# An attention and MLP kernel: mirrored score blocks turned by VectorE and DMA, and an addition moved to GpSimd

## The chip, the cores and the metric

The kernel runs on one core of a Trainium2 chip. The metric is the device time of one launch in microseconds (us), as the median of several runs. TensorE multiplies, VectorE and ScalarE work on tiles in SBUF (on-chip memory) and PSUM (TensorE's results), GpSimd works on tiles in SBUF, and SyncE issues every DMA of this kernel.

## The reference

The input x has 8 batches of 1024 rows and 256 features. All is float32.

```
h = layernorm(x) * (1 + ca) + sa                 # ca, sa, ga, cb, sb, gb: per batch, from a small matmul
scores = (h * w_lhs) @ (h * w_rhs).T             # 1024 x 1024 per batch
x = x + ga * (softmax(scores, axis=2) @ h)
h = layernorm(x) * (1 + cb) + sb
x = x + gb * (relu(h @ W1 + b1) @ W2 + b2)       # W1: 256 x 1024, W2: 1024 x 256
```

Both factors of the scores are the same rows scaled by feature, so scores[s, t] = scores[t, s]: the score matrix of a batch is symmetric. This is what lets a block be copied from its mirror image.

## The kernel before

The 1024 rows of a batch are 8 tiles of 128, so the scores are 8 by 8 blocks of 128 by 128. In every batch but the first a product is made from split operands: x is cut into a high part (fp32r, names ending in `hi`) and the rest (`lo`), and each product is three matmuls, hi by hi, hi by lo, lo by hi. With two halves of the 256 features a score group is six matmuls. The first batch multiplies float32 operands directly.

Work is named by steps, and each engine runs its own hand-planned list of them, in order: `FIRST_STEPS` (batch 0), `SECOND_STEPS`, `STEPS` (the loop over batches 2 to 6), `LAST_STEPS` and `AFTER_STEPS`. A step with a minus belongs to the batch before, one with a plus to the next. So the MLP of one batch, the attention of the next and the normalisation of a third are interleaved. The steps that matter here:

- `SC.n` (lines 560 to 585, 864): TensorE makes row tile n of the scores in `score[n % 2]` (PSUM); VectorE copies it to `S` and takes the row maxima into `row_max` in the same instruction. Tiles 0 to 3 have all 8 column blocks, tiles 4 to 7 only the 4 right ones. Within the upper left 4 by 4 blocks and within the lower right 4 by 4, the blocks below the diagonal are turned by TensorE (`nc.tensor.transpose`, line 584) from blocks already in `S`, 5 in each; `first_col` makes 11 of 16 be multiplied. With the 16 upper right blocks that is 38 multiplied blocks and 10 turned by TensorE.
- `ST`, `SW`, `SR` and `MX`: the 16 lower left blocks are not made on TensorE. VectorE transposes 32 by 32 pieces of the upper right blocks into `stage` (`ST`, line 896), SyncE stores them to memory (`SW`) and reads them back in turned order into `lower` (`SR`); `MX` (lines 900 and 903) takes their row maxima.
- `MB`: TensorE turns the row maxima into rows in `max_ps`, which is `score[1]` (line 655). `SB.n` (lines 887 to 892): VectorE subtracts the maxima in place in `S`. `EX`: ScalarE's exponential, in place. `SM`: ScalarE writes `Phi` (the high part), VectorE `Plo` (line 911); both are rings of three slots. `AV.n`: TensorE multiplies them with `V`, 24 matmuls; VectorE adds the result to `x_cur` and takes statistics.
- `F.n`, `G.n` (16 each per batch): first and second layer of the MLP. ScalarE makes `hid` and `hid_hi`, and GpSimd `hid_lo` (line 1088), which TensorE needs for the last third of `G.n`. Six matmuls of 512 columns make an `F`, twelve of 256 a `G`.
- `L1`, `L2` (statistics), `N1`, `N2` (normalised rows to `ln_t`), `BH`, `B2`, `TH`, `T2` (turning them by features through VectorE and DMA), `XC` (GpSimd adds the modulation to `x_cur`, line 1139), and `XG` (line 1051): VectorE adds the gated bias `gb_b2` to `x_cur` and writes `x_mlp`.

TensorE's waits that matter: `SC.n` waits until score tile n - 2 is read (`scores_read`), and a turned block until its source is in `S`:

```python
for i in range(left // P, at // P):
    if i == at // P - 1:
        pe.wait_ge(scores_read, T * b + i + 1)
    last = nc.tensor.transpose(score[n % 2][:, i * P:(i + 1) * P], S[:, i, n * P:(n + 1) * P], ident[:])
```

`MB.1` waits for `MX`; `G` waits for `hid_hi` and `hid_lo`; `AV` for `Phi` and `Plo`.

## Time and profile before

| what | value |
|---|---|
| median of 3 runs | 693.37 us (692.94 to 694.24) |
| profiled execution, span from first to last instruction | 691.5 us |
| busy: TensorE, VectorE, ScalarE, GpSimd | 686.1, 558.4, 427.5, 361.7 us |
| TensorE's granted clock, mean | 1.000 (the 2.4 GHz level) |
| DMA | 77.54 MB, 112 GB/s |

The span leaves out what lies before the first and after the last instruction. Busy time of TensorE is from modelled ends of pipelined matmuls, so what a matmul costs is read from the distance between the starts of two, not from its duration.

### The profile page before, as it was taken

Reading aid. Unit: us, or ns where it says so; the run is one execution under the profiler, and the core shown is the slowest. Engines: PE = TensorE matmul, PEld = TensorE weight load, DVE = VectorE, ACT = ScalarE, POOL = GpSimd, SP = SyncE. Lnnn points to the kernel's source line nnn. Section 1 sums busy time; section 2 is a strip of 40 time slices with the busy share of each in tenths; the row PEclk is TensorE's granted clock in tenths of the full one; section 3 lists DMA queues with packets and bytes.
Section 4 is the critical chain, followed back from the end, with each engine's and each line's share of the span. In section 5 each row is a group of like instructions: output and inputs, shape, how many; then the busy total and the mean of one; then the engine's idle time right before and its main releaser. Section 6 shows DMA issues by size and latency. Waiting matters only on the chain.

```text
span 691.5 us, 13488 instructions
## 1 busy us (share of the span) xinstructions
PE 686.1 (99%) x4621; PEld 627.7 (91%) x4621; DVE 558.4 (81%) x1059; ACT 427.5 (62%) x625; POOL 361.7 (52%) x396
## 2 busy tenths in 40 slices
...
GB/s 294 81 49 59 204 193 55 39 107 252 123 100 56 103 232 91 99 61 179 180 67 90 67 226 185 61 38 98 258 121 99 46 91 221 1 1 100 100 31 30
DMA packets 61663, 77.54 MB, mean 112 GB/s; under 512 B 5632, under 2 KB 54336, under 8 KB 61632
## 3 DMA queue, kind: packets, MB, share of 16 engines
...
q14 instruction: 13, 0.11, 0.1%
HBM read 46.15 MB, written 30.97 MB: 112 GB/s over the span
## 4 chain that ended last, share of the span: by engine, by line
PE 94%; DVE 4%; issue 0%; ACT 0%; DMA 0%; DVEq 0%; ACTq 0%; SPq 0%
PE col L595 9%; PE col L594 9%; PE col L593 9%; PE acc L530 8%; PE acc L531 8%; PE acc L536 8%; PE score L694 8%; PE score L690 8%; PE score L691 8%; PE score L578 4%; PE score L579 4%; PE score L580 4%; PE score L576 2%; PE score L584 2%; PE score L499 1%; DVE S L879 1%
## 5 line engine op out<-in xcount | busy, mean ns | idle before, releaser
L1088 POOL TENSOR_TENSOR hid_lo<-hid,hid_hi 128x512 fp32r<-128x512 f32 x127 | 175.4, 1386 | 143.2 <-ACT hid_hi L719 142.8
L715 ACT ACTIVATE hid<-col,b1T 128x512 f32<-128x512 f32 x128 | 87.0, 679 | 140.3 <-PE col L595 126.1
L530 PE MATMUL acc<-W2hi,hid_hi 128*128 128x256 f32 x480 | 119.2, 282 | 0.0
L531 PE MATMUL acc<-W2lo,hid_hi 128*128 128x256 f32 x480 | 116.9, 278 | 0.0
L690 PE MATMUL score<-V,Phi 128*128 128x258 f32 x448 | 108.8, 281 | 0.0
L691 PE MATMUL score<-V,Phi 128*128 128x256 f32 x448 | 108.6, 281 | 0.0
L719 ACT ACTIVATE hid_hi<-hid 128x512 fp32r<-128x512 f32 x128 | 81.0, 633 | 37.6 <-PE acc L536 29.8
L593 PE MATMUL col<-h2hi,W1hi 128*128 128x512 f32 x256 | 102.4, 400 | 0.0
L595 PE MATMUL col<-h2hi,W1lo 128*128 128x512 f32 x256 | 101.0, 395 | 0.0
L594 PE MATMUL col<-h2lo,W1hi 128*128 128x512 f32 x256 | 100.6, 393 | 0.0
L530 PEld LDWEIGHTS acc<-W2hi,hid_hi 128*128 128x128 f32 x480 | 90.4, 188 | 2.1
L531 PEld LDWEIGHTS acc<-W2lo,hid_hi 128*128 128x128 f32 x480 | 90.2, 188 | 1.8
L690 PEld LDWEIGHTS score<-V,Phi 128*128 128x128 f32 x448 | 85.0, 190 | 0.7
L691 PEld LDWEIGHTS score<-V,Phi 128*128 128x128 f32 x448 | 84.0, 188 | 0.6
L1069 POOL TENSOR_SCALAR nm<-mv 128x4 f32<-128x4 f32 x32 | 16.7, 523 | 129.2 <-DVE mv L932 104.2
L911 DVE TENSOR_TENSOR Plo<-S,Phi 128x1024 fp32r<-128x1024 f32 x56 | 70.2, 1269 | 8.1 <-ACT Phi L806 6.4
L536 PE MATMUL acc<-W2hi,hid_lo 128*128 128x256 f32 x480 | 76.6, 276 | 0.0
L864 DVE TENSOR_SCALAR_CACHE_REDUCE S<-score 128x1024 f32<-128x1024 f32 (+1 forms) x64 | 62.7, 980 | 15.2 <-PE score L584 12.9
L793 ACT ACTIVATE S<-S 128x1024 f32<-128x1024 f32 (+1 forms) x64 | 64.4, 1019 | 13.2 <-DVE S L879 7.7
L1139 POOL TENSOR_TENSOR x_cur<-x_cur,attn_mod 128x512 f32<-128x512 f32 x32 | 43.3, 1354 | 40.8 <-DVE ln_v L1038 40.8
L536 PEld LDWEIGHTS acc<-W2hi,hid_lo 128*128 128x128 f32 x480 | 64.6, 188 | 0.0
L694 PE MATMUL score<-V,Plo 128*128 128x258 f32 x448 | 62.8, 282 | 0.0
...
## 6 DMA issues: line engine op xcount, KB each, us to landing
block_rows<-blocks SPq DMA_DIRECT2D x29, 512.0 KB, 2.9
blocks<-block_rows SPq DMA_DIRECT2D x116, 128.0 KB, 3.0
x_cur<-x SPq DMA_DIRECT2D x16, 512.0 KB, 3.9
ln_t<-x SPq DMA_DIRECT2D x14, 512.0 KB, 4.8
score_blocks<-stage SPq DMA_DIRECT2D x14, 512.0 KB, 4.2
lower<-score_blocks SPq DMA_DIRECT2D x56, 128.0 KB, 2.9
out<-x_mlp SPq DMA_DIRECT2D x8, 512.0 KB, 3.0
...
```

The lines of the kernel that those rows point to most:

```text
L530: nc.tensor.matmul(o, hi, W2hi[:, it, :], start=(it == 0 and (apart or t % 2 == 0)), stop=False, skip_group_check=True)
L531: nc.tensor.matmul(o, hi, W2lo[:, it, :], start=False, stop=False, skip_group_check=True)
L536: last = nc.tensor.matmul(o, lo, W2hi[:, it, :], start=False, stop=(it == FT - 1), skip_group_check=True)
L593: nc.tensor.matmul(col[n % 2][:], W1hi[:, kk, tile], h2hi[:, kk, cols], start=(kk == 0), stop=False)
L594: nc.tensor.matmul(col[n % 2][:], W1hi[:, kk, tile], h2lo[:, kk, cols], start=False, stop=False)
L595: last = nc.tensor.matmul(col[n % 2][:], W1lo[:, kk, tile], h2hi[:, kk, cols], start=False, stop=(kk == DK - 1))
L690: nc.tensor.matmul(o, Phi[:, slot, t, :], V[:, t, 0:VW], start=(t == 0), stop=False)
L691: nc.tensor.matmul(o[:, 0:D], Phi[:, slot, t, :], V[:, t, VP:VP + D], start=False, stop=False)
L694: last = nc.tensor.matmul(o, Plo[:, slot, t, :], V[:, t, VP:VP + VW], start=False, stop=(t == T - 1))
L715: nc.scalar.activation(hid[:, n % 2, :], col[n % 2][:], ACT.Relu, bias=b1T[:, n % FT:n % FT + 1]).then_inc(col_read, 1)
L719: nc.scalar.activation(hid_hi[:, n % RING, :], hid[:, n % 2, :], ACT.Copy).then_inc(hid_hi_done, 1)
L1088: G.tensor_tensor(hid_lo[:, n % RING, :], hid[:, n % 2, :], hid_hi[:, n % RING, :].bitcast(F32), ALU.subtract).then_inc(hid_lo_done, 1)
```

## The change

The upper left and lower right 4 by 4 blocks of the scores now have 10 multiplied blocks each, and TensorE turns none (the first batch excepted). The 6 mirrored blocks of each go the way of the lower left ones: `QT` (VectorE, 32 by 32 transposes into `stage_q`), `QW` (store to `quarter_blocks`), `QR` (four reads back). All blocks are packed into `S`; `lower` now lies in `S` too. `SB` no longer works in place: it writes to `soft`, a ring of three slots that lies where `Plo` lies, in three instructions for each row tile. The row maxima are put together from parts (`part_max`), in `MX.0` (upper half, now needed before `MB.0`), `MX.1` (`lower`) and `MX.2` (lower half). `XG` goes from VectorE to GpSimd. All step lists are written anew. The loop's lists, and the first batch's where it matters:

```diff
 FIRST_STEPS
     "pe": """
-        SC.0 MF.2 MF.3 SC.1 MD.0 SC.2 SC.3 SC.4 MB.0 SC.5 SC.6 SC.7 AU.0 AU.1 MB.1 AV.0 AV.1 AV.2 AV.3 AV.4 AV.5
-        AV.6 TP.0 WR.0 AV.7
+        MF.2 SC.0 MF.3 SC.1 MD.0 SC.2 SC.3 SC.4 MB.0 SC.5 SC.6 SC.7 AU.0 MB.1 AU.1 AV.0 AV.1 AV.2 WR.0 AV.3
+        AV.4 AV.5 AV.6 AV.7 TP.0
     "dve": """
-        SC.0 MF.0 L1.0+ SC.1 GA.0 SC.2 BH.0+ SC.3 SC.4 SU.0 SU.1 SC.5 SU.2 SC.6 SC.7 SB.0 SB.1 SU.3 SB.2
+        L1.0+ SC.0 MF.0 BH.0+ GA.0 SC.1 SC.2 SC.3 L1.1+ SC.4 SU.0 SC.5 SC.6 SU.1 SC.7 SU.2 SB.0 SB.1 SB.2 SB.3
 STEPS
     "pe": """
-        SC.0 F.0- SC.1 F.1- F.2- SC.2 SC.3 F.3- SC.4 F.4- MB.0 G.0- SC.5 G.1- SC.6 F.5- SC.7 G.2- F.6- G.3-
-        G.4- F.7- G.5- F.8- F.9- G.6- F.10- MB.1 G.7- AV.0 F.11- AV.1 G.8- F.12- G.9- AV.2 G.10- AV.3 F.13-
-        F.14- AV.4 F.15- G.11- AV.5 G.12- AV.6 G.13- G.14- G.15- AV.7
+        SC.0 SC.1 F.0- F.1- SC.2 SC.3 SC.4 F.2- F.3- SC.5 SC.6 G.0- F.4- SC.7 G.1- F.5- F.6- G.2- G.3- MB.0
+        F.7- G.4- G.5- G.6- G.7- F.8- F.9- F.10- AV.0 G.8- F.11- AV.1 MB.1 G.9- F.12- AV.2 AV.3 AV.4 F.13-
+        G.10- G.11- F.14- AV.5 G.12- F.15- G.13- AV.6 G.14- AV.7 G.15-
     "act": """
+        F.0- VN.0 F.1- T2.1- V.0 F.2- F.3- F.4- VN.1 F.5- V.1 F.6- F.7- EX.0 EX.1 L1.0+ SM.0 F.8- SM.1 F.9-
+        EX.2 F.10- SM.2 EX.3 SM.3 TH.0+ F.11- EX.4 SM.4 EX.5 SM.5 F.12- EX.6 F.13- TH.1+ F.14- EX.7 SM.6 F.15-
+        SM.7 MC.0 T2.0
     "dve": """
-        SC.0 B2.1- ST.0 SC.1 XG.2- ST.1 VL.0 XG.3- SC.2 L1.0+ SC.3 ST.2 ST.3 SC.4 V.0 T2.1- SC.5 SB.0 SB.1
-        SC.6 SC.7 BH.0+ SB.2 VL.1 SM.0 MX.0 SB.3 V.1 L1.1+ SM.1 SB.4 OUT.0- AV.0 BH.1+ SB.5 AV.1 SM.2 SM.3
-        SM.4 TH.0+ SM.5 AV.2 AV.3 SB.6 XG.0 AV.4 B2.0 SB.7 SM.6 TH.1+ AV.5 AV.6 SM.7 T2.0 XG.1 AV.7 OUT.1-
+        B2.1- SC.0 SC.1 ST.0 SC.2 VL.0 SC.3 ST.1 QT.0 ST.2 SC.4 L1.0+ SC.5 SC.6 T2.1- ST.3 SC.7 QT.1 MX.0 V.0
+        VL.1 BH.0+ SB.0 SB.1 MX.1 V.1 SM.0 OUT.0- SM.1 SB.2 L1.1+ MX.2 SB.3 AV.0 SM.2 SM.3 AV.1 BH.1+ SB.4
+        AV.2 SB.5 SM.4 SB.6 AV.3 TH.0+ SB.7 SM.5 B2.0 TH.1+ AV.4 SM.6 AV.5 SM.7 AV.6 AV.7 T2.0 OUT.1-
     "pool": """
-        N2.1- XC.0 F.0- XC.1 F.1- F.2- L1.0+ F.3- N1.0+ F.4- F.5- F.6- XC.2 F.7- F.8- F.9- L1.1+ N1.1+ F.10-
-        F.11- F.12- L2.0 N2.0 XC.3 F.13- F.14- F.15- L2.1
+        N2.1- XG.2- XG.3- F.0- F.1- XC.0 F.2- XC.1 L1.0+ N1.0+ F.3- F.4- F.5- F.6- F.7- F.8- L1.1+ F.9- F.10-
+        N1.1+ F.11- XG.0 L2.0 XG.1 N2.0 XC.2 F.12- F.13- F.14- F.15- XC.3 L2.1
     "sp": """
+        AM.0 S2.1- R2.1- XT.0+ GB.0 X1.0 QW.0 QR.0 SW.0 SW.1 QW.1 SR.0 SR.1 SH.0+ GA.0- RH.0+ XT.1+ QR.1 SH.1+
+        O0.0- RH.1+ S2.0 R2.0 O1.0- X0.0+ O1.1-
 AFTER_STEPS
     "dve": """
-        B2.1- XG.2- XG.3- T2.1- OUT.0- F.15- OT.0-
+        B2.1- T2.1- OUT.0- F.15- OT.0-
     "pool": """
+        N2.1- F.0- F.1- XG.2- XG.3- F.2- F.3- F.4- F.5- F.6- F.7- F.8- F.9- F.10- F.11- F.12- F.13- F.14-
```

The code, cut to its core:

```diff
+    QCOLS = [(0, 1, 2), (1, 2, 3), (2, 3), (0, 3)]
+    UPPER, TURNS = 26, 6
+    PACKED = [0, 3, 6, 8]
+    MAX_ORDER = [3, 0, 1, 2]
...
+                        quarter = QCOLS[n % HT]
+                        for right in range(0 if n < HT else 1, 2):
+                            if right and n == 0:
                                 wait(pe, av_read, T * b)
+                            if not right:
+                                o = score[n % 2][:, 0:HR]
+                            else:
+                                o = score[n % 2][:, HR:HR + len(quarter) * P]
...
-                        for i in range(left // P, at // P):
-                            if i == at // P - 1:
-                                pe.wait_ge(scores_read, T * b + i + 1)
-                            last = nc.tensor.transpose(score[n % 2][:, i * P:(i + 1) * P], S[:, i, n * P:(n + 1) * P], ident[:])
                         last.then_inc(scores_done, 1)
...
                     elif kind == "MB":
-                        pe.wait_ge(scores_read, T * b + HT * (n + 1))
-                        if ph is not PH["first"] and n == 1:
-                            pe.wait_ge(max_ready, b)
+                            pe.wait_ge(max_ready, 2 * b + n - 1)
...
                     elif kind == "SB":
+                        tile, h, t = soft[:, n % RING, :, :], n // HT, n % HT
+                        dve.wait_ge(av_done, T * b + max(n - RING + 1, 0))
...
+                        V_.tensor_tensor(tile[:, h * HT:(h + 1) * HT][:, rows], kept, most.broadcast_to(list(kept.shape)), ALU.subtract)
...
+                        V_.tensor_tensor(by_quarter(out), turned_q[h][:, turns], by_quarter(most.broadcast_to(list(out.shape))), ALU.subtract)
...
+                            V_.tensor_tensor(tile[:, 0:HT], s_upper[:, :, t, :], most.broadcast_to([P, HT, P]), ALU.subtract).then_inc(sub_done, 1)
...
+                    elif kind == "QT":
+                        dve.wait_ge(scores_read, T * b + (n + 1) * HT)
...
+                        V_.transpose(stage_q[n].rearrange("p (u g j r) -> p g j u r", u=Q, g=3, j=2),
+                                     pairs.rearrange("p g j (u r) -> p g j u r", r=QP)).then_inc(quarter_done[n], 1)
+                    elif kind == "MX" and n == 1:
+                        wait_apart(dve, scores_turned[0], 16 * Q * b)
+                        dve.wait_ge(scores_turned[1], 16 * Q * b)
+                        by_row = lower.rearrange("p h u v t r -> p v (h u) (t r)")
+                        V_.tensor_reduce(part_max[:, 1, 3, 0:3], by_row[:, 1:HT], AX.XY, ALU.max)
+                        V_.tensor_reduce(part_max[:, 1, 3, 3:4], by_row[:, 0:1], AX.XY, ALU.max).then_inc(left_done, 1)
                     elif kind == "MX":
+                        h = n // 2
+                        dve.wait_ge(quarter_turned[h], 16 * Q * b)
...
+                        V_.tensor_reduce(places.rearrange("p j g -> p g j"), turned_q[h].rearrange("p (g j) u r -> p g j u r", j=2), AX.XY, ALU.max).then_inc(parts_done, 1)
...
+                        dve.wait_ge(parts_done, 2 * b + h - 1)
+                        V_.tensor_reduce(row_max[:, h * HT:(h + 1) * HT], part_max[:, h].rearrange("p k a -> p a k"), AX.X, ALU.max).then_inc(max_ready, 1)
...
+                    elif kind == "XG":
...
+                        pool.wait_ge(av_read, T * batch + 2 * n + 2)
+                        G.tensor_tensor(x_mlp[:, 2 * n:2 * n + 2, :], x_cur[:, 2 * n:2 * n + 2, :],
+                                        gb_b2[:].unsqueeze(1).broadcast_to([P, 2, D]), ALU.add).then_inc(xg_done, 1)
```

## Rows read from the trace of the kernel before

**Rows 1.** The page: busy time of each engine, and the chain that ended last.

```profile
PE 686.1 (99%) x4621; PEld 627.7 (91%) x4621; DVE 558.4 (81%) x1059; ACT 427.5 (62%) x625; POOL 361.7 (52%) x396
...
PE 94%; DVE 4%; issue 0%; ACT 0%; DMA 0%; DVEq 0%; ACTq 0%; SPq 0%
```

**Rows 2.** One period of the loop: busy us (instructions) by engine, clock, DMA share.

```profile
276.00:358.60 82.60, 82.60 (x576) 76.72 (x575) 71.89 (x133) 54.98 (x81) 45.02 (x49) 1.00 0.38 121
```

**Rows 3.** The timeline of TensorE in batch 4 (from 0): start, duration, line, form.

```profile
319.21 0.34 PE L578 MATMUL score<-Rhi,Lhi 128*128 128x384 f32 x1
...
320.26 0.39 PE L578 MATMUL score<-Rhi,Lhi 128*128 128x512 f32 x1
...
321.64 0.27 PE L584 MATMUL score<-ident,S 128*128 128x128 f32 x1
...
326.61 0.38 PE L584 MATMUL score<-ident,S 128*128 128x128 f32 x2
...
326.95 0.28 PE L579 MATMUL score<-Rlo,Lhi 128*128 128x256 f32 x1
```

**Rows 4.** VectorE's groups by form: busy time, mean ns of one, then idle before.

```profile
L864 DVE TENSOR_SCALAR_CACHE_REDUCE S<-score 128x1024 f32<-128x1024 f32 x36 | 43.7, 1214 | 6.6 <-PE score L584 4.4 <-PE score L576 2.2
L887 DVE TENSOR_TENSOR S<-S,score 128x1024 f32<-128x1024 f32 x28 | 33.3, 1195 | 1.0 <-PE score L655 1.0
...
L1051 DVE TENSOR_TENSOR x_mlp<-x_cur,gb_b 128x512 f32<-128x512 f32 x32 | 24.8, 782 | 3.0 <-DMA out<-x_mlp 3.0
...
L864 DVE TENSOR_SCALAR_CACHE_REDUCE S<-score 128x512 f32<-128x512 f32 x28 | 19.0, 680 | 8.6 <-PE score L584 8.5
L896 DVE STREAM_TRANSPOSE stage<-S 128x512 f32<-128x512 f32 x28 | 19.0, 693 | 0.1
L892 DVE TENSOR_TENSOR S<-lower,score 128x512 f32<-128x512 f32 x28 | 19.0, 677 | 3.9 <-DMA lower<-score_blocks 3.9
...
L900 DVE TENSOR_REDUCE left_max<-lower 128x4 f32<-128x2048 f32 x7 | 15.9, 2272 | 0.0
```

**Rows 5.** GpSimd's groups by form.

```profile
L1088 POOL TENSOR_TENSOR hid_lo<-hid,hid_hi 128x512 fp32r<-128x512 f32 x127 | 175.4, 1386 | 143.2 <-ACT hid_hi L719 142.8
L1139 POOL TENSOR_TENSOR x_cur<-x_cur,attn_mod 128x512 f32<-128x512 f32 x32 | 43.3, 1354 | 40.8 <-DVE ln_v L1038 40.8
L1079 POOL TENSOR_SCALAR ln_t<-x_cur,nm,rs 128x256 f32<-128x256 f32 x64 | 37.8, 606 | 3.4 <-POOL rs L1072 2.3 <-issue 1.0
L1072 POOL TENSOR_TENSOR rs<-var_eps,half_power 128x4 f32<-128x4 f32 x32 | 35.6, 1112 | 2.7
```

**Rows 6.** The timeline of VectorE in batch 4.

```profile
370.58 1.78 DVE L997 SCALAR_TENSOR_TENSOR Llo<-featT,wl,Lhi 128x512 fp32r<-128x512 f32 x1
```

**Rows 7.** The timeline of GpSimd at that time.

```profile
370.09 1.72 POOL L1088 TENSOR_TENSOR hid_lo<-hid,hid_hi 128x512 fp32r<-128x512 f32 x1 [2.78 <-ACT hid_hi L719]
```

**Rows 8.** The page: DMA issues, with KB each and microseconds to landing.

```profile
score_blocks<-stage SPq DMA_DIRECT2D x14, 512.0 KB, 4.2
lower<-score_blocks SPq DMA_DIRECT2D x56, 128.0 KB, 2.9
```

**Rows 9.** The timeline of VectorE in the first batch.

```profile
22.60 1.39 DVE L951 BATCH_NORM_STATS2 stats<-ln_t 128x6 f32<-128x256 f32 x4
...
28.47 0.71 DVE L990 STREAM_TRANSPOSE blocks<-ln_t 128x512 f32<-128x512 f32 x1
```

**Rows 10.** The timeline of TensorE in the first batch.

```profile
24.22 2.75 PE L576 MATMUL score<-R_first,L_first 128*128 128x256 f32 x8
26.81 0.38 PE L584 MATMUL score<-ident,S 128*128 128x128 f32 x2
```

**Rows 11.** Tile ln_t in batch 0: first DMA issue, and times to landing.

```profile
L400 SPq DMA_DIRECT2D ln_t<-x x1: 3960/3960/3960, 6.9 to 6.9; - x1
...
DMA to landing us min/median/max: 4.0/8.3/12.6
```

**Rows 12.** The timeline of TensorE's weight loads at the second batch's start.

```profile
69.38 0.19 PEld L578 LDWEIGHTS score<-Rhi,Lhi 128*128 128x128 f32 x1 [0.55 <-DVE x_cur L926]
```

More of the change, by code:

```diff
@@ L339, in block_kernel @@
         scores_done, scores_read = sem("scores_done"), sem("scores_read")
+        parts_done = sem("parts_done")
         max_done, left_done, max_ready = sem("max_done"), sem("left_done"), sem("max_ready")
-        stage_done, stage_stored, scores_turned = sem("stage_done"), sem("stage_stored"), sem("scores_turned")
+        stage_done, stage_stored, scores_turned = sem("stage_done"), [sem("stage_stored0"), sem("stage_stored1")], [sem("scores_turned0"), sem("scores_turned1")]
+        quarter_done, quarter_stored, quarter_turned = [[sem(f"quarter_{what}{h}") for h in range(2)] for what in ("done", "stored", "turned")]
         sub_done, exp_done, phi_done, plo_done = sem("sub_done"), sem("exp_done"), sem("phi_done"), sem("plo_done")
@@ L559, in part @@
                             pe.wait_ge(scores_read, T * b + n - 1)
[L560 to L570 removed]
+                        tile = slice(n * P, (n + 1) * P)
@@ new lines, in part @@
+                        if ph is PH["first"]:
+                            at = first_col[n]
+                            for lo_col in range(0, ROWS, HR):
+                                start_col = max(at, lo_col)
+                                width = lo_col + HR - start_col
+                                if width <= 0 or n == 0 and lo_col == 0:
+                                    continue
+                                o, cols = score[n % 2][:, start_col:lo_col + HR], slice(start_col, lo_col + HR)
+                                for kk in range(DK):
+                                    last = nc.tensor.matmul(o, L_first[:, kk, tile], R_first[:, kk, cols], start=(kk == 0), stop=(kk == DK - 1))
+                            for i in range(at // P):
+                                if i == at // P - 1:
+                                    pe.wait_ge(scores_read, T * b + i + 1)
+                                last = nc.tensor.transpose(score[n % 2][:, i * P:(i + 1) * P], S[:, i, n * P:(n + 1) * P], ident[:])
+                            last.then_inc(scores_done, 1)
+                            continue
```

233 lines of the change are left out of this document (133 added, 100 removed).

## The prediction

> **What bounds the kernel now.** I read the page first, for who is busy and what the last chain is made of: TensorE is busy 99% of the span and makes 94% of the chain [rows 1]. Both could hide short waits, because ends of matmuls are modelled, so the second view is a window of about one loop period: TensorE 82.60 of 82.60 us at clock 1.00, VectorE 71.9, GpSimd 45.0 [rows 2]. The third is the timeline inside a batch, where starts follow each other in fixed steps with no wait between them [rows 3]. So in the loop the time is TensorE's instruction list, and each nanosecond taken from that list is won, as long as what feeds TensorE stays ahead of it. VectorE has some 10.7 us of idle time in a period to do so, GpSimd 37.6.
>
> **TensorE's list.** Six matmuls of 384 columns run from 319.21 to 320.26, 0.175 us each, and six of 512 from 320.26 to 321.64, 0.230 each [rows 3]; by that line one of 256 takes 0.12. The change narrows the right group of `SC.0` and the only group of `SC.4` from four blocks to three: 12 matmuls by 0.055 = 0.66 us per batch. The other tiles keep their widths (3 and 4, 2 and 4, 2 and 4, 3, 2, 2 blocks); that the two blocks of `SC.3` and `SC.7` now lie apart I cost at nothing, since the columns stream at the same count, and at up to 12 matmuls by 0.06 = 0.7 if the gap costs half. The ten transposes go: two and the 256-column matmul behind them take 326.61 to 326.95, 0.34 less 0.12, so 0.11 each [rows 3], 1.10 us per batch. Together 1.76, in seven batches 12.3 us. Both parts lie on TensorE's own list, so nothing has to be found that they uncover. If the transposes were hidden in some pipeline, only 4.6 would be left; the starts say that they aren't.
>
> **VectorE's load.** Lengths by the rows of 512 and 1024 elements, which give about 0.16 us plus 1.03 ns per element [rows 4]. `SC`: four of 1.214 and four of 0.680, 7.58, become 896, 896, 768, 512 and 256, 384, 384, 256, 256 elements: 6.1, so -1.5. `QT`: two transposes of 768, by the row of 693 ns for 512 0.95 each, +1.9 (its four-step pattern could make it 1.8 each, +3.6). `MX`: 2.27 and a small one become 768 twice, 1536, 512 and two small ones, +2.3. `SB`: 4 x 1.35 + 4 x 1.195 = 10.2 become eight of three pieces (0.84 for the two short ones, 0.68), 12.2, +2.0. `XG`: 4 x 0.78 leave, -3.1. Net +1.6 us: 73.5 busy in a period of 80.8. It fits, with 7 us left where 10.7 were.
>
> **GpSimd's load.** Four `XG` at the 1.354 of its other addition of the same shape [rows 5] are +5.4: 50.4 of 80.8. None of it is on TensorE's path by itself; what is queued behind each is. `XG.2` and `XG.3` stand ahead of the first `F`, and TensorE wants that hid_lo only in `G.0`, after seven score tiles and four `F`. `XG.1` is different, see below.
>
> A GpSimd instruction can also hold VectorE up. One `Llo` of 512 columns with two SBUF inputs took 1.78 us [rows 6] while GpSimd worked from 370.09 to 371.81 [rows 7]; the `XG` on VectorE, of the same size with two such inputs, takes 0.78 [rows 4]. So a moved `XG` may give VectorE up to 1.0 us of delay each, 4.0 per period at worst, 0 at best. I take 1 to 2 us per period, inside the 7 left. The Trainium skill has this as a rule (SBUF — State Buffer, section "SBUF: two separate sides"): GpSimd and a VectorE instruction with two SBUF inputs lock one port pair and the loser waits for the whole of the other; the 1.78 agrees with it. By that rule moving additions between the two engines wins VectorE less than its 3.1 us, which speaks against this part of the change.
>
> **The waits that the change adds.** Times from the start of `SC.0`: `F` is six 512-column matmuls, 1.38; `G` twelve of 256, 1.4; `AV` 24 of 256, 2.9.
> - `MB.0` now waits for turned blocks. TensorE reaches it after 12.6 us of scores, seven `F` and four `G`: 27.9. `QT.0` stands behind the read of `SC.3`, done at about 15; the store lands 4.2 later and the reads, 2.9 to land [rows 8] with some 1.5 for issuing four, at 23.6; `MX.0` ends at 24.8. Slack 3. Behind `MX.0` on VectorE stand `V.0`, `VL.1`, `BH.0` and `SB.0`; a late landing would push them all.
> - SyncE gets two stores and eight reads more per batch, placed ahead of `SH.0+`, `RH.0+`; the only one in a hurry is `QR.0`, above. DMA is at a share of 0.38 [rows 2] and gets 1.5 MB more per batch on about 10. I cost it at nothing.
> - `MB.1` comes at 48.1. From `MB.0` on VectorE has about 17 us of listed work up to `MX.2`, and waits for ScalarE's `SM.1` in it: 45. Slack 3.
> - `G.12` is the tightest. GpSimd's list there is `L2.0 XG.1 N2.0 XC.2 F.12-`, and `L2.0` waits for the statistics of `AV.3`. From the end of `AV.3` VectorE has `SM.4`, `SB.6` and its own step, about 4 us; then GpSimd needs at least 1.1, 1.35, four of 0.61, 1.35 and 1.39 [rows 5], 7.6. TensorE wants hid_lo two thirds into `G.12`: `AV.4`, four steps, `AV.5` and 0.9, 12.3 us after `AV.3`. 11.6 against 12.3: slack 0.7. `XG.1` alone is 1.35 of this. ScalarE's `F.14` waits for the same hid_lo, and behind it `EX.7` and `SM.6` for `AV.6`.
> - The ring `soft`: `SB.n` waits for `AV.n-3`, as `Phi` and `Plo` did; at least two `AV` and two `F` or `G` lie between, 8 us, for a chain of 1.5 + 1.0 + 1.0 + 1.2. It costs nothing.
>
> **First and last batch.** In the first, `L1.0+` and `BH.0+` are moved ahead of the reads of `SC.0` and `SC.1`. The first `ln_t` load is issued at 6.85, and with the longest landing of 12.6 [rows 11] is there at 19.5. From its statistics to the transpose of `BH` took 28.47 - 22.60 = 5.9 us [rows 9], so `BH.0` can start at 25.4, ends at 26.7, `GA.0` follows, and `SC.1` is read by 28.2. TensorE wants that for the transposes of `SC.2`, which ran at 26.81 behind eight matmuls from 24.22 [rows 10]. So 1.4 us are lost; up to 3 if `L1.1+`, moved ahead of the read of `SC.4`, is late too; 0 if the load lands in the shortest 4.0. Given back at its end: 0.55 us in which TensorE waited for the read of `AV.7` [rows 12] are filled by `TP.0`, now behind it. Net +0.9 (-0.6 to +2.5). In the last part `G.0` waits for `XG.3`, now behind `N2.1`, two `F` and `XG.2` on GpSimd, 8 us against six `F`, 8.3: nothing, at worst 1.
>
> **Sum.** -12.3 + 0.9 = -11.4. The profiled span is 691.5, so 680.1; the median of the runs lies 1.9 above the span, and so 682.0 is the forecast.
>
> **Rivals.**
> - A, the list shrinks and TensorE stays fed: 682.0, own range 680.3 to 684. Chance 0.62.
> - B, one place per period slips, `G.12` most likely, because `XG.1` or VectorE blocked behind GpSimd eats its slack of 0.7. For it: the 1.78 [rows 6]. Against it: one slip moves TensorE, and all that waits on it gains the same slack, so a period loses once. Six or seven periods by 0.4 to 1.3 us: 684.5 to 690.5. Chance 0.25. This is what the Trainium skill's rule above would make of it.
> - C, slower: VectorE becomes the bound between `QT.1` and `SB.4`. Its 7 us left must be used up and 1.76 more: this takes `QT` at 1.8 each (+1.7), the reduces at twice their 2.3 (+2.3), the short pieces of `SB` at twice their length (+4), and blocking over 1 us. All of it with 3 us of blocking is +11.0, a period of 84.5 us, 1.9 more than the 82.6 of before, seven times: 693.4 + 13.3, about 707. It decides from +9.1 (7.3 left and 1.76). Against it: all rows of these forms lie on one line per element [rows 4]. Chance 0.07.
> - D, only the narrower matmuls count: the transposes' 7.7 stay as some other wait, 689.7. Chance 0.04.
> - E, more than the sum: under 680.3, where the first batch loses nothing and its end wins. Chance 0.02.
>
> **How the numbers follow.** A change of 0.2%, 1.4 us, is about what a measurement of this kernel can tell from none. Faster takes A, B, D, E and little of C: 0.92; same 0.03; slower 0.05. The range leaves out C, E and the top of B: 680.3 to 688.
>
> **What the profile would show.** Right: no transposes on TensorE between the scores after the first batch; 168 score matmuls of 384 columns where 84 were; starts in the same steps of 0.23, 0.175, 0.12; the period shorter by 1.7 to 1.8 us; `XG` on GpSimd at about 1.35 and VectorE at 73 to 76 per period. Wrong: steps between TensorE's starts of over 0.4 us, in `G.12` (waiting for hid_lo), at `MB.0` or `MB.1` (for `MX`), or in `AV` (for `Plo`); in the first batch a pause before the transposes of `SC.2` shows that term. What would upset the forecast most is GpSimd late by over a microsecond in every batch, or `QT` and `MX` far above their lines.

## The result and the profile after

The change makes the kernel slower: 760.6 us median of four runs (759.3 to 761.5), against 693.3 of the kernel before on the same chip (692.9 to 694.2). The ratio is 1.096 [1.0945, 1.0979], 67 us more where 11 less were forecast. The profiled execution has a span of 757.5 us and a mean granted clock of 0.982.

The page of the changed kernel, busy time by engine and what the last chain is made of, answers to [rows 1]:

```profile
PE 699.6 (92%) x4551; PEld 633.7 (84%) x4551; DVE 615.7 (81%) x1168; ACT 429.8 (57%) x625; POOL 422.5 (56%) x428
...
PE 8%; POOL 1%; DVE 0%; issue 0%
```

The chain that was TensorE to 94% breaks off after 9% of the span. TensorE's share of busy time is 92%, with fewer instructions, and the engine now has pauses. VectorE's load rose by 57.3 us, 8.2 a batch. One period, from 250 us, and then three slices of 5 us in it (columns as in [rows 2]):

```profile
250.00:340.70 90.70, 83.39 (x564) 75.99 (x563) 81.47 (x149) 55.20 (x81) 53.37 (x53) 1.00 0.41 127
330.00:335.00 5.00, 3.33 (x28) 3.14 (x28) 3.03 (x4) 1.67 (x3) 5.00 (x7) 1.00 0.18 72
335.00:340.00 5.00, 3.11 (x21) 2.67 (x21) 4.84 (x6) 4.86 (x8) 3.76 (x3) 1.00 0.41 138
340.00:345.00 5.00, 5.00 (x31) 5.00 (x31) 4.63 (x8) 2.78 (x4) 1.47 (x2) 0.66 0.00 0
```

TensorE's list was 82.60 of 82.60 busy; now a period takes about 91 us. TensorE's timeline over that window, the rows that carry a wait (in brackets the idle time before, and its releaser):

```profile
252.20 1.22 PE L746 MATMUL score<-V,Plo 128*128 128x258 f32 x8 [0.73 <-DVE Plo L1015]
...
277.21 0.38 PE L629 MATMUL score<-Rhi,Lhi 128*128 128x256 f32 x1 [1.19 <-DVE S L931]
...
288.50 0.74 PE L569 MATMUL acc<-W2hi,hid_lo 128*128 128x256 f32 x4 [0.43 <-POOL hid_lo L1183]
294.38 0.38 PE L563 MATMUL acc<-W2hi,hid_hi 128*128 128x256 f32 x1 [0.57 <-ACT hid_hi L771]
...
320.27 0.39 PE L742 MATMUL score<-V,Phi 128*128 128x258 f32 x1 [0.57 <-ACT Phi L864]
334.36 0.73 PE L569 MATMUL acc<-W2hi,hid_lo 128*128 128x256 f32 x4 [1.67 <-POOL hid_lo L1183]
339.74 0.38 PE L742 MATMUL score<-V,Phi 128*128 128x258 f32 x1 [1.89 <-DVE x_cur L1032]
```

With one of 0.18 at 295.76, eight waits make 7.2 us. Six kinds of feeder are late in one period: `Plo`, the read of a score tile, `hid_lo`, `hid_hi`, `Phi` and `x_cur`. Two in a row, in `G.12` and at `AV.6`, leave TensorE idle for 3.6 us of ten; from 340 to 345 the granted clock is 0.66, so part of that slice ran at 1.2 GHz and not at 2.4 (the starts of `AV.6`'s matmuls are 0.12 us apart up to 340.4 and 0.21 behind it). Over the whole kernel TensorE's waits after 60 us sum to 48 us, where the kernel before shows none. The mean clock of 0.982 stands for at most 14 us more (757.5 x 0.018); before it was 1.000. What was late there is seen on GpSimd and VectorE:

```profile
324.75 0.52 POOL L1164 TENSOR_SCALAR nm<-mv 128x4 f32<-128x4 f32 x1 [1.70 <-DVE mv L1036]
325.34 0.60 POOL L1165 TENSOR_SCALAR var_eps<-mv 128x4 f32<-128x4 f32 x1
326.02 1.40 POOL L1167 TENSOR_TENSOR rs<-var_eps,half_power 128x4 f32<-128x4 f32 x1
327.40 1.30 POOL L1244 TENSOR_TENSOR x_mlp<-x_cur,gb_b 128x512 f32<-128x512 f32 x1
328.70 3.14 POOL L1174 TENSOR_SCALAR ln_t<-x_cur,nm,rs 128x256 f32<-128x256 f32 x4
331.80 1.28 POOL L1234 TENSOR_TENSOR x_cur<-x_cur,attn_mod 128x512 f32<-128x512 f32 x1
333.04 4.68 POOL L1183 TENSOR_TENSOR hid_lo<-hid,hid_hi 128x512 fp32r<-128x512 f32 x3
```

```profile
331.97 0.71 DVE L1094 STREAM_TRANSPOSE blocks<-ln_t 128x512 f32<-128x512 f32 x1 [2.18 <-POOL ln_t L1174]
332.61 0.67 DVE L1095 STREAM_TRANSPOSE blocks<-ln_t 128x512 f32<-128x512 f32 x1
333.20 1.65 DVE L1101 SCALAR_TENSOR_TENSOR Llo<-featT,wl,Lhi 128x512 fp32r<-128x512 f32 x1
334.77 1.78 DVE L1103 SCALAR_TENSOR_TENSOR Rlo<-featT,wr,Rhi 128x512 fp32r<-128x512 f32 x1
336.48 1.78 DVE L1101 SCALAR_TENSOR_TENSOR Llo<-featT,wl,Lhi 128x512 fp32r<-128x512 f32 x1
338.19 0.74 DVE L1103 SCALAR_TENSOR_TENSOR Rlo<-featT,wr,Rhi 128x512 fp32r<-128x512 f32 x1
```

The reader is to see one chain run back and forth. `L2.0` waits for VectorE's statistics, `XG.1` and a slow `N2.0` follow it, VectorE stands 2.18 us at `B2.0` for that `ln_t`, GpSimd's overdue `hid_lo` burst then runs beside VectorE's `TH.1` and three of its four operations take 1.65 to 1.78 us where the last, beside an idle GpSimd, takes 0.74; the read of `AV.4` behind them is late, and `AV.6` waits for its bank. VectorE's groups by form, for [rows 4], and GpSimd's, for [rows 5]:

```profile
L1015 DVE TENSOR_TENSOR Plo<-soft,Phi 128x1024 fp32r<-128x1024 f32 x56 | 86.1, 1546 | 3.0 <-ACT Phi L864 2.9
L1142 DVE SCALAR_TENSOR_TENSOR ln_v<-ln_v,rs,attn_mod 128x256 f32<-128x256 f32 x56 | 52.9, 1003 | 6.6 <-ACT ln_v L835 5.5 <-DMA attn_mod<-mod_rows 1.1
...
L1006 DVE TENSOR_REDUCE part_max<-S 128x6 f32<-128x768 f32 x14 | 12.9, 925 | 0.0
L999 DVE TENSOR_REDUCE part_max<-S 128x3 f32<-128x1536 f32 x7 | 12.2, 1736 | 0.0
...
L992 DVE STREAM_TRANSPOSE stage_lr<-S 128x768 f32<-128x768 f32 x7 | 6.8, 975 | 0.2
```

```profile
L1174 POOL TENSOR_SCALAR ln_t<-ln_t,nm,rs 128x256 f32<-128x256 f32 x56 | 47.2, 854 | 1.3 <-POOL rs L1167 1.3
...
L1244 POOL TENSOR_TENSOR x_mlp<-x_cur,gb_b 128x512 f32<-128x512 f32 x32 | 44.2, 1390 | 37.2 <-DMA out<-x_mlp 37.2
```

The new operations have the lengths that were forecast (925, 1736, 975 ns; `XG` 1390). The old ones grew. In the same view of the kernel before `Plo` has a mean of 1269 ns and `ln_v` of 498:

```profile
L911 DVE TENSOR_TENSOR Plo<-S,Phi 128x1024 fp32r<-128x1024 f32 x56 | 70.2, 1269 | 8.1 <-ACT Phi L806 6.4 <-issue 0.8
...
L1038 DVE SCALAR_TENSOR_TENSOR ln_v<-ln_v,rs,attn_mod 128x256 f32<-128x256 f32 x56 | 24.5, 498 | 0.5 <-ACT ln_v L783 0.4
```

These two alone are 44.3 us more, at the same count and shape.

In the first batch the forecast term is there. TensorE waits before the second transpose of `SC.2`, for the read of `SC.1`, where none was [rows 10]:

```profile
28.39 0.33 PE L607 MATMUL score<-ident,S 128*128 128x128 f32 x1 [1.07 <-DVE S L924]
...
54.12 12.19 PE L735 MATMUL score<-V_unsplit,S 128*128 128x258 f32 x48 [3.43 <-POOL W2lo L1211]
...
73.90 0.48 PE L629 MATMUL score<-Rhi,Lhi 128*128 128x512 f32 x1
```

The last row is the first score matmul of batch 1. It came at 67.64 before, so the first batch lost 6.3 us, and the wait at `SC.2` is the smaller part of it; the larger is 3.43 us for `W2lo`, in the row between, and behind it the granted clock is 0.66 from 53 to 58 us, some 1.7 us more. From there to the first score matmul of batch 7 the kernel takes 549.0 us for 495.6, 8.9 a period, and from that to its end 134.6 for 128.3. Together 66.0 us, the whole difference of the spans.

### The profile page after: what moved, and what is told of

Same layout as the page of the kernel before. It is cut to its first block and busy times, and to the rows that moved or that the text cites. A ratio compares the mean times of both kernels' runs of the same rounds, so it can differ in the third digit from the quotient of the medians.

```text
span 757.5 us, 13573 instructions
## 1 busy us (share of the span) xinstructions
PE 699.6 (92%) x4551; PEld 633.7 (84%) x4551; DVE 615.7 (81%) x1168; ACT 429.8 (57%) x625; POOL 422.5 (56%) x428
## 5 line engine op out<-in xcount | busy, mean ns | idle before, releaser
L742 PE MATMUL score<-V,Phi 128*128 128x258 f32 x448 | 112.7, 288 | 11.7 <-DVE x_cur L1032 9.4
L743 PE MATMUL score<-V,Phi 128*128 128x256 f32 x448 | 111.8, 286 | 0.0
L742 PEld LDWEIGHTS score<-V,Phi 128*128 128x128 f32 x448 | 87.2, 195 | 14.9 <-issue 10.6
L569 PE MATMUL acc<-W2hi,hid_lo 128*128 128x256 f32 x480 | 79.9, 284 | 13.9 <-POOL hid_lo L1183 13.7
L1015 DVE TENSOR_TENSOR Plo<-soft,Phi 128x1024 fp32r<-128x1024 f32 x56 | 86.1, 1546 | 3.0 <-ACT Phi L864 2.9
L743 PEld LDWEIGHTS score<-V,Phi 128*128 128x128 f32 x448 | 86.5, 193 | 1.1
L1164 POOL TENSOR_SCALAR nm<-mv 128x4 f32<-128x4 f32 x32 | 12.8, 399 | 129.8 <-DVE mv L1036 76.6
L848 ACT ACTIVATE soft<-soft 128x1024 f32<-128x1024 f32 x56 | 58.5, 1053 | 44.1 <-DVE soft L978 24.2
L746 PE MATMUL score<-V,Plo 128*128 128x258 f32 x448 | 65.2, 289 | 5.8 <-DVE Plo L1015 5.8
L629 PE MATMUL score<-Rhi,Lhi 128*128 128x512 f32 (+2 forms) x168 | 58.3, 347 | 8.5 <-DVE S L931 5.0
L1244 POOL TENSOR_TENSOR x_mlp<-x_cur,gb_b 128x512 f32<-128x512 f32 x32 | 44.2, 1390 | 37.2 <-DMA out<-x_mlp 37.2
```

Of the source, the lines that this page charges most:

```text
L569: last = nc.tensor.matmul(o, lo, W2hi[:, it, :], start=False, stop=(it == FT - 1), skip_group_check=True)
L742: nc.tensor.matmul(o, Phi[:, slot, t, :], V[:, t, 0:VW], start=(t == 0), stop=False)
L743: nc.tensor.matmul(o[:, 0:D], Phi[:, slot, t, :], V[:, t, VP:VP + D], start=False, stop=False)
L1015: V_.tensor_tensor(Plo[:, n % RING, :, :], soft[:, n % RING, :, :], Phi[:, n % RING, :, :].bitcast(F32), ALU.subtract).then_inc(plo_done, 1)
```

## The experiments

Three theories were put to the chip: the additions on GpSimd hold the others up (1); the new scheme for the scores does, with its turned quarters and VectorE's added load (2); the new order of the steps does, on all five queues (3). The diff rewrites the order lists together with the scheme, so they had to be taken apart. All runs were timed beside the kernel before, which lay between 693.6 and 694.1 each time.

**The additions.** First the changed kernel with `XG` back on VectorE, and the kernel before with `XG` on GpSimd:

```diff
-"dve":  ... SC.1 ST.0 SC.2 VL.0 ...
-"pool": N2.1- XG.2- XG.3- F.0- ... F.11- XG.0 L2.0 XG.1 N2.0
+"dve":  ... SC.1 XG.2- ST.0 SC.2 VL.0 XG.3- ... SM.5 XG.0 ... SM.7 XG.1
+"pool": N2.1- F.0- ... F.11- L2.0 N2.0
```

> The changed kernel, with the gated bias added on VectorE again (at the places that correspond to the old ones) and everything else as changed. Theory 1: moving the addition to GpSimd is what makes it slow, because it stands in GpSimd's queue waiting for a store, and the work behind it then comes in bursts that hold up VectorE's instructions with two SBUF inputs. Then most of the 67 us come back: 685 to 710 us, and the mean of the ln_v instruction falls from 1003 ns towards 500. Theory 2: the turned blocks and the subtraction out of place cost it, through VectorE and the DMA. Then it stays at 745 or above. Theory 3: the new order of steps on all engines costs it, whoever adds the bias. Then it stays above 735 as well, with the same places of waiting.

Measured: 751.4 us (749.3 to 757.8), 9.2 less than the changed kernel; ratio to before 1.085 [1.080, 1.091]. Its trace has one wait that the changed kernel has at 1.80 us only: `F.0-` in batch 2's list waits 9.19 us for `h2lo`. TensorE's, VectorE's and SyncE's rows:

```profile
174.12 0.79 PE L640 MATMUL col<-h2hi,W1hi 128*128 128x512 f32 x1 [9.19 <-DVE h2lo L1106]
```

```profile
159.87 0.66 DVE L1156 TENSOR_TENSOR x_mlp<-x_cur,gb_b 128x512 f32<-128x512 f32 x1
```

```profile
160.56 0.40 SPq L496 DMA_DIRECT2D x_cur<-x  x1
161.39 0.34 SPq L429 DMA_DIRECT2D block_rows<-blocks  x1
```

In batch 1's new list for SyncE the load `X0.0+` stands ahead of the store `S2.0`, and it waits for `XG.1`, here the row at 159.87. The blocks that `S2.0` stores had been turned at 152.7, so store, reads and `h2lo` all come some 8 us late. In the old list `S2.0` stood first. From batch 3 to batch 6 this run's periods are 89.5 us long, against 91.0 in the changed kernel.

> The kernel before, with the gated bias added on GpSimd alone, at the corresponding places of GpSimd's list (behind N2.1, ahead of L2.0 and ahead of N2.0); in the last batch SyncE's bias load and first store stand earlier, so that nothing waits in a circle. Theory 1: 725 to 770 us. Theories 2 and 3: 693 to 705.

Measured: 697.7 us, ratio 1.005 [1.003, 1.007]. VectorE's groups in this run, against a `Plo` of 1269 ns before:

```profile
L910 DVE TENSOR_TENSOR Plo<-S,Phi 128x1024 fp32r<-128x1024 f32 x56 | 79.0, 1425 | 1.7 <-issue 0.8
L996 DVE SCALAR_TENSOR_TENSOR Llo<-featT,wl,Lhi 128x512 fp32r<-128x512 f32 x28 | 32.2, 1148 | 0.0
```

Then the additions cut to 8 of 256 columns, with their steps and waits in place, and in another run the additions behind the next `F` steps:

```diff
-G.tensor_tensor(x_mlp[:, 2 * n:2 * n + 2, :], x_cur[:, 2 * n:2 * n + 2, :],
+G.tensor_tensor(x_mlp[:, 2 * n:2 * n + 2, 0:8], x_cur[:, 2 * n:2 * n + 2, 0:8],
```

```diff
-"pool": N2.1- XG.2- XG.3- F.0- F.1- ... XG.0 L2.0 XG.1 N2.0 ... F.14- F.15-
+"pool": N2.1- F.0- F.1- XG.2- XG.3- ... L2.0 N2.0 ... F.14- XG.0 F.15- XG.1
```

> The changed kernel, with the addition on GpSimd cut to 8 of 256 columns of each tile, all its waits kept. It leaves out most of the bias and residual, so the output is not that of the reference. If the length and port of the addition cost the time, it falls to 700 to 720. If its wait for the store, and what queues behind it, costs the time, it stays at 740 or more. If theory 2 or 3 holds, it stays above 745.

Measured: 742.1 us, ratio 1.068 [1.063, 1.072].

> The changed kernel, with the addition on GpSimd placed where its waits are over: XG.2 and XG.3 behind the first two F, XG.0 and XG.1 behind F.14 and F.15. Theory 1 by the wait for the store: 710 to 735. Theory 1 by the length and port alone: 745 to 765. Theory 2 or 3: above 745.

Measured: 764.0 us, ratio 1.102 [1.098, 1.106]. The first lies in the range of the wait for the store (740 or more), and the second, which takes that wait away, speaks against it (710 to 735); so neither wait nor length is shown as the cause. The additions cost the changed kernel 9 us on GpSimd against VectorE, 18 against hardly being there. The 9 between the additions on VectorE (751.4) and the short ones (742.1) is about the one wait of 9.19 us, which is 0.42 with the short additions; so with `XG.1` or `X0.0+` placed otherwise the additions on VectorE might win up to twice the 9, an estimate that no run tests. Theory 1 holds for 9 to 18 of 67, and the other place that was tried for them doesn't help.

**Scheme against order.** The new scheme with the order lists of before, its new steps put in by hand, and the old scheme with the new lists, less the steps that it doesn't have; both with `XG` on VectorE. The first is the old order as far as the scheme lets it be: both `MB` and several subtractions and exponentials stand later than before, because the maxima are ready later, and batches 1 and 7 use the loop's lists, where the kernel before has lists of their own. VectorE's list of the first, between the scores and the maxima:

```diff
-B2.1- SC.0 SC.1 ST.0 SC.2 VL.0 SC.3 ST.1 QT.0 ST.2 SC.4 L1.0+ ... ST.3 SC.7 QT.1 MX.0
+SC.0 B2.1- ST.0 SC.1 XG.2- ST.1 VL.0 XG.3- SC.2 L1.0+ SC.3 QT.0 ST.2 ST.3 SC.4 ... SC.7 QT.1 MX.0
```

> The changed kernel's scheme (36 multiplied blocks, turned quarters, soft out of place) with the bias on VectorE, under the step lists of the kernel before, to which only the new steps are added: QT, QW, QR, MX.0, MX.2, MB.0 behind F.6, MB.1 behind AV.0, SB.3 to SB.5 behind AV.0 to AV.2; the loop's lists serve batches 1 and 7 too. Theory 2 (the scheme costs it, whatever the order): 725 or more. Theory 3 (the new order of the steps costs it): 680 to 697, with few waits on TensorE.

Measured: 703.9 us, ratio 1.014 [1.012, 1.015], above the range of theory 3 and far below that of theory 2.

> The kernel before in its scheme (38 multiplied blocks, ten turned by TensorE, subtraction in place), bias on VectorE, under the step lists of the changed kernel without QT, QW, QR, MX.0 and MX.2 (MX at the place of MX.1, in the last batch ahead of SM.1). Theory 2: 690 to 712. Theory 3: 730 to 755, with TensorE waiting in the same places (G for hid_lo, AV for x_cur) as the changed kernel.

Measured: 767.2 us, ratio 1.104 [1.101, 1.106], above theory 3's range too. The four corners, `XG` on VectorE in all:

| | old order | new order |
|---|---|---|
| old scheme | 693.4 | 767.2 |
| new scheme | 703.9 | 751.4 |

The order costs 74 us with the old scheme and 47 with the new. Theory 2 falls as the main cause, theory 3 stands. Three things in the traces bear on the sizes. The mean clocks of the right column are 0.964 and 0.982, so at most 28 of the 74 and 12 of the 47 us are clock. The wait behind `X0.0+` is in both: 9.19 us with the new scheme, and 10.98 in `SC.1`, behind the same late `h2lo`, with the old. And where the old scheme has the new order, what TensorE waits for most is not what the changed kernel waits for: the view of its waits (sum, times, longest) has the turned blocks, which the new scheme doesn't make on TensorE, in front.

```profile
PE score L583 <- DVE S L863: 23.6, 10, 11.0
```

So the 47 is the figure for the changed kernel, and the 74 shows that an order made for one scheme is dearer still under the other. In the run with the new scheme and old order the longest of the waits left is plain, at `MB.0`, by SyncE's queue and VectorE's timeline:

```profile
416.21 1.73 SPq L471 DMA_DIRECT2D S<-score_blocks  x4
...
418.70 0.38 SPq L476 DMA_DIRECT2D quarter_blocks<-soft  x1
419.89 0.33 SPq L466 DMA_DIRECT2D score_blocks<-stage  x1
424.66 1.75 SPq L482 DMA_DIRECT2D S<-quarter_blocks  x4
```

```profile
428.31 0.95 DVE L1006 TENSOR_REDUCE part_max<-S 128x6 f32<-128x768 f32 x1 [1.46 <-DMA S<-quarter_blocks]
```

The quarter's reads go out at 424.66, and `MX.0` stands for them; TensorE waited 1.41 us there. The next two runs take the order apart. The changed kernel with the first batch's lists of before:

> The changed kernel with the first batch's step lists of the kernel before (XG.0 and XG.1 on GpSimd at its end). From the start of batch 1's scores, 6 us later than before, 5 to 7 us should come back: 753 to 757. If the first batch's order has no part in it, 760.

Measured: 751.1 us, ratio 1.083 [1.078, 1.089]; the first batch's order is worth 9 us (the four runs lie between 747.4 and 755.7), its own 6.3 and some of what follows. And the first run's kernel (751.4) with the old order for GpSimd and SyncE alone:

```diff
-"pool": N2.1- F.0- F.1- XC.0 F.2- XC.1 L1.0+ N1.0+ F.3- ... F.11- L2.0 N2.0 XC.2 F.12-
+"pool": N2.1- XC.0 F.0- XC.1 F.1- F.2- L1.0+ F.3- N1.0+ ... F.12- L2.0 N2.0 XC.3 F.13-
```

> The changed kernel with the additions on VectorE (751.4 us), with GpSimd's and SyncE's lists of batches 1 to 7 taken from the run with the old order (703.9 us); the lists of TensorE, ScalarE and VectorE stay those of the change. If the new places of L1, N1, XC and N2 on GpSimd and of the loads and stores in SyncE's queue are what makes the new order slow, the time falls to 710 to 725 us. If it is the order on TensorE, ScalarE and VectorE (scores in runs of three, seven F and G steps between them and AV.0), the time stays within 5 us of 751. Theory: it stays, 745 to 755 us.

Measured: 796.3 us, ratio 1.149 [1.147, 1.150]. Both theories missed it, by over 40 us: the five lists are one schedule, and two of them from another are worse than either. TensorE's longest waits are now for ScalarE's `hid`, 32.7 us, and the mean clock is 0.955.

**Load or places.** The first run's kernel again, with the maxima cut so that VectorE has less to do and every step stays:

```diff
-V_.tensor_reduce(part_max[:, 1, 3, 0:3], by_row[:, 1:HT], AX.XY, ALU.max)
+V_.tensor_reduce(part_max[:, 1, 3, 0:3], by_row[:, 1:HT, :, 0:4], AX.XY, ALU.max)
```

> The changed kernel with the additions on VectorE (751.4 us, period about 89 us) with every reduction of the maxima cut to 4 of 32 rows of each turned quarter: the four reductions of a batch (2 x 0.93, 1.74, 0.67 us) fall to under 0.3 us each, which takes some 3.5 us a batch off VectorE and leaves every step, wait and DMA in place. It leaves out most of the search for the row maxima, so the subtracted maxima are not the real ones. If VectorE's load is what TensorE waits for in the new order, most of it comes back: 3 us a batch, 727 to 735 us. If it is the order itself (chains across engines in which each waits for the other's step in turn), little comes back: 743 to 751 us. Theory: between, nearer the second, 740 to 748 us.

Measured: 748.7 us, ratio 1.079 [1.077, 1.081]. VectorE's groups, for the 925 and 1736 ns above:

```profile
L1006 DVE TENSOR_REDUCE part_max<-S 128x6 f32<-128x96 f32 x14 | 3.3, 238 | 5.3 <-DMA S<-quarter_blocks 5.3
L999 DVE TENSOR_REDUCE part_max<-S 128x3 f32<-128x96 f32 x7 | 1.7, 241 | 1.5 <-DMA S<-score_blocks 1.5
```

With 0.69 x 2 + 1.50 + 0.50 = 3.4 us a batch taken off VectorE, 2.7 us came back of 58. VectorE's load isn't the bound in this order, as far as the maxima can show it. Next, two of the places:

```diff
-"dve":  ... B2.0 TH.1+ AV.4 SM.6 AV.5 SM.7 ...
-"pool": ... F.11- L2.0 N2.0 XC.2 F.12- F.13- F.14- ...
+"dve":  ... B2.0 AV.4 SM.6 AV.5 TH.1+ SM.7 ...
+"pool": ... F.11- L2.0 N2.0 F.12- F.13- XC.2 F.14- ...
```

> The changed kernel with the additions on VectorE (751.4 us) and two moves in the lists of batches 2 to 6: VectorE's second TH behind AV.5's read (TensorE waited 2.0 us a batch for AV.5's x_cur at AV.7, while the four Llo and Rlo took 1.7 us each beside three hid_lo on GpSimd) and GpSimd's XC.2 behind F.13 (TensorE waited 1.3 us a batch for hid_lo at the G step ahead of AV.6). If the waits that the trace names are the cause, five batches give back 3 us each: 734 to 740 us. If slack is missing everywhere in this order, the wait moves to the next step and 2 to 6 us come back: 745 to 750. Theory: in between, 738 to 746 us.

Measured: 747.3 us, ratio 1.077 [1.075, 1.079]; 4 us back of the 16 of the two waits. (By TensorE's list the wait that the expectation puts at `AV.7` is that of `AV.6`, for the read of `AV.4`, the first behind `TH.1`; the move takes both reads ahead of `TH.1`.) TensorE's waits for `x_cur` at `AV.6`, 9.4 us in the kernel, and those in `G.12` are gone. Its waits for `Plo` went from 2.8 to 10.9 us, and for the maxima from 1.8 to 5.1. And waits stand at steps where the run of 751.4 had none over 0.25 us in the same batch:

```profile
345.46 1.22 PE L746 MATMUL score<-V,Plo 128*128 128x258 f32 x8 [1.32 <-DVE Plo L1015]
...
356.12 0.50 PE L629 MATMUL score<-Rhi,Lhi 128*128 128x512 f32 x1 [0.41 <-DVE S L934]
...
409.86 0.39 PE L742 MATMUL score<-V,Phi 128*128 128x258 f32 x1 [0.58 <-ACT Phi L864]
```

Slack is short all along this order: a wait taken away comes out at the next step, for the most part.

**The old order mended.** Where the run of 703.9 us waited, its lists were changed: the quarter's store and reads ahead of the half block's, `SM.7` and `AV.5` earlier, `XG.0` and `XG.1` later, `MB.0` behind `G.3`, and `AV.7` of the last batch before the last `G` steps.

```diff
-"sp":  ... R2.1- SR.0 X1.0 QW.0 SW.1 QR.0 SR.1 QW.1 ...
-"dve": ... SB.6 XG.0 SM.5 AV.4 B2.0 SB.7 SM.6 TH.1+ AV.5 AV.6 SM.7 T2.0 XG.1 AV.7 OUT.1-
+"sp":  ... R2.1- X1.0 QW.0 QR.0 SR.0 SW.1 QW.1 SR.1 ...
+"dve": ... SB.6 SM.5 AV.4 SB.7 B2.0 SM.6 AV.5 TH.1+ SM.7 AV.6 T2.0 XG.0 XG.1 AV.7 OUT.1-
```

> The new scheme with the additions on VectorE and the lists of the kernel before, mended where the run with the old order still waited. That run took 703.9 us; its TensorE waits over 0.25 us summed to 18.7 us after 60 us, against 2.1 in the kernel before: 6.8 at the first group of maxima, 6.8 at the attention's second halves (Plo), 2.3 behind the last batch. Mended: the first quarter store and load are issued ahead of the other block's load (QW.0 QR.0 before SR.0, SW.1), MB.0 stands behind G.3, AV.5's read before the second TH, SM.7 ahead of AV.6's read, both late additions behind the last subtraction, and in the last batch AV.7 stands ahead of three G steps. Theory: the scheme does shorten TensorE's list by 1.76 us a batch (12.3 us) and only waits hid it; then removing some 14 of the 16.6 us of added waits gives 688 us (684 to 693). Rival: VectorE, which is busy without a gap from QT.1 to AV.7 in the run with the old order, has become the bound there (my rival C); then the waits reappear at another step and the time stays at 698 to 705 us.

Measured: 701.6 us, ratio 1.011 [1.010, 1.013]; the rival's time. Beside it, the same with `XG` on GpSimd:

> The run before this one in the list, with the gated bias added on GpSimd as in the changed kernel (XG.2 and XG.3 behind N2.1, XG.0 ahead of L2.0, XG.1 ahead of N2.0, the same places as in the kernel before with only this part of the change, which took 697.7 us, 4 us more). If VectorE is the bound in the stretch of the subtractions, taking 2.8 us a batch away from it gives back up to 7 x 0.7 us: 3 to 5 us faster than its neighbour. If the two engines' delays to one another weigh more, as they did there and in the changed kernel (9 us), it is 4 to 9 us slower than its neighbour. Theory: slower, 692 to 697 us if its neighbour takes 688.

Measured: 712.8 us, ratio 1.031 [1.026, 1.037], 11 us more. TensorE's waits for `Plo` went from 2.8 to 15.2 us.

In the trace of 701.6 us VectorE stood 1.66 us before `SC.7` in a stretch that was full behind it, and in the last batch TensorE waited 2.90 us for a `Phi` that ScalarE made behind a hidden block. So once more:

```diff
-"dve": ... SC.6 SC.7 QT.1 ... SB.2 VL.1 SM.0 ... T2.0 XG.0 XG.1 AV.7 OUT.1-
-"act": ... F.12- EX.4 SM.4 EX.5 SM.5 F.13- F.14- EX.6 SM.6 F.15- EX.7 SM.7 MC.0 T2.0
+"dve": ... SC.6 VL.1 SC.7 QT.1 ... SB.2 SM.0 ... XG.0 T2.0 AV.7 XG.1 OUT.1-
+"act": ... F.12- EX.4 SM.4 MC.0 EX.5 SM.5 EX.6 SM.6 F.13- EX.7 SM.7 F.14- T2.0 F.15-
```

(ScalarE's only in the last batch, where TensorE's `AV.7` also moved ahead of four `G` steps.)

> The mended order (701.6 us) mended again where it still waits. Its period is 82.3 us with 1 to 1.5 us of waits in it, and it loses 5 us in the last batch against the kernel before (3.0 at the attention's Phi, ScalarE standing at a late hidden block, 0.8 behind it). Now the last batch has ScalarE's EX.6, SM.6, EX.7 and SM.7 ahead of F.14 and TensorE's AV.7 ahead of four G steps; in each batch VL.1 stands in VectorE's idle 1.7 us before SC.7, AV.7's read ahead of XG.1, and MB.0 ahead of G.3 again. Theory: the scheme is worth about 1.3 us a batch on TensorE once nothing waits, and the rest is order; then the time is 690 to 695 us (4 to 5 us from the last batch, 0.5 to 1 a batch from VectorE's stretch). Rival: VectorE is the bound between QT.1 and AV.7 whatever stands there; then the period stays at 82.3 and the time at 696 to 699 us.

Measured: 689.5 us, ratio 0.993 [0.9915, 0.9948]: 4.2 us faster than the kernel before, and just under the range expected. One period of it (columns as in [rows 2]):

```profile
258.83:340.35 81.52, 80.95 (x560) 75.24 (x560) 75.71 (x153) 55.28 (x80) 44.43 (x49) 1.00 0.48 142
```

At last this best order with `XG` on GpSimd, as late in its list as it goes:

> The best order so far (689.5 us, period 81.35 us, waits over 0.25 us of 8.6 in all) with the additions on GpSimd, XG.0 and XG.1 at the end of its list, XG.2 and XG.3 behind N2.1. In the order before it, which still waited for VectorE, the move cost 11.2 us (712.8 against 701.6). If VectorE's delays by GpSimd are what costs (four more operations of 1.3 us that take VectorE's time beside them), it costs the same here: 698 to 703 us. If GpSimd's own lateness was the cost (XG ahead of N2), the end of the list makes it cheaper: 690 to 695 us. Theory: 694 to 700 us.

Measured: 694.5 us, ratio 1.000 [0.999, 1.002]: 5.0 us more than with `XG` on VectorE. `Llo` has a mean of 1061 ns here and 851 there, `Rlo` 965 against 744.

## Why the prediction was wrong

Its terms of what the engines execute came out for the most part; its way of deciding whether TensorE stays fed did not.

- **The step that failed** is "The waits that the change adds". It looked for the semaphores that are new and summed slack for five places (`MB.0` 3 us, `MB.1` 3, `G.12` 0.7), with each instruction at the duration that it has alone. The diff moves nearly every step on all five queues, and this was costed at nothing outside those places. The runs show that it is the main part of the matter: with the additions on VectorE the new lists cost the new scheme 47 us over the old ones (751.4 against 703.9), and the old scheme, where no quarter has to be turned, 74.
- **"One slip moves TensorE, and all that waits on it gains the same slack, so a period loses once"**, by which rival B ended at 690.5. It doesn't hold: a period has eight waits, 7.2 us, and the chain above shows feeders that wait for each other. `G.12` was rightly named as one that slips, by 1.67, but the 1.89 at `AV.6` behind it had no term; in `G.12` the chain from `L2.0` through `XC.2` takes 333.04 - 324.75 = 8.3 where 6.2 of the 7.6 forecast were meant for it (1.1, 1.35, 2.44 and 1.35).
- **Blocking between GpSimd and VectorE** was taken at 1 to 2 us a batch. `Plo`, `ln_v`, `Llo`, `Rlo` and `h2lo` together are busy 226.5 us after (86.1, 52.9, 31.6, 26.0, 29.9) and 164.6 before: 61.9 us, 8.8 a batch. Most isn't from `XG`: with it on VectorE the same five still take 202.6. Of these 38 us more than before, `ln_v` has 11.9 and `Plo` 10.6. `ln_v`'s come of the places (its mean is 472 ns in the new scheme with the old order), among them a burst of `hid_lo`; `Plo`'s don't, or not alone, since it has a mean of 1451 ns in that run too. And it was weighed as load against VectorE's idle time, while it acts as delay at single steps; the cut maxima show that 3.4 us of load a batch hardly count. The rule of the Trainium skill (SBUF — State Buffer, section "SBUF: two separate sides") was cited for the 1.78 and then priced for the moved additions alone; the rows of 1.65 and 1.78 beside `hid_lo` agree with it, and it bears on every VectorE instruction with two SBUF inputs that the new order brings beside a GpSimd step.
- **TensorE's list**, 1.76 us a batch. Mechanism right: 26 transposes are left, 168 score matmuls have 384 columns, and the period without waits is shorter. Size too large. By differences of starts on TensorE's timeline, before a batch's score matmuls take 13.3 us and its transposes 0.6; in the best run the matmuls take 12.7 (five periods). So the narrower matmuls give 0.6, as forecast (0.66), and the transposes 0.6 and not 1.10: the pair on which their 0.11 rests was a slow one. It's 1.2 a batch, 8.4 us and not 12.3.
- **The first batch**, +0.9. The wait at `SC.2` came, 1.07 for 1.4. The 3.43 us for GpSimd's `WS.0` did not figure: it went behind `N1.1` while `WR.0`, which needs it, went ahead of `AV.3`, and I read neither move. With the first batch's old lists the first score matmuls of batch 1 are back before 68 us.
- **VectorE's load**, the lengths: right within 5% for `QT`, `MX`, `SC` and the pieces of `SB`. The sum of +1.6 us a batch became +8.2, mostly by the blocking above. **GpSimd's**: right, 1390 for 1354 ns.
- **The rivals.** C had the sign and not the mechanism: VectorE isn't the bound in the changed kernel. In the mended old order it comes near: with `VL.1` moved into VectorE's idle time, and the late additions out of its fullest stretch, the period fell from 82.3 to 81.4. On the transposes the truth lies midway between A (1.10 us a batch) and D (nothing): 0.6.

What is shown: the order is the main cause, the additions cost 9 us more, the scheme itself wins once fed (4 us measured). The win is the scheme's and not only the new lists': six periods take 489.4 us in the best run and 495.6 before, where the view of TensorE's waits shows none that another order could have taken away. Behind them 2.9 us are lost again. Not settled is which of the moved steps of TensorE, ScalarE and VectorE starts the lateness in the loop; these three were only run together. The 14 us between the 703.9 and the 689.5 are mended waits, not traced one by one.
